# Keys and values of blocks 2 to 7 made transposed and turned back on TensorE, and fewer, moved looks at the weights

## The chip, the cores and the metric

The kernel runs on one core of one Trainium2 chip. The metric is the time of one execution on the device in microseconds (us). Three executions of the kernel before took 650.98, 651.08 and 651.11 us; the median is 651.08.

## The reference

One layer of attention without a softmax, and a feed-forward network with gates, each with a residual and a layer norm behind it, on 4096 tokens of width 256:

```
Q, K, V = x Wq^T, x Wk^T, x Wv^T              # width 64 each
energy  = K^T V                               # 64 x 64
out     = (Q energy) * sqrt(3/64) Wo^T
x       = layernorm(x + out)
h = silu(x W1^T * s1) * (x W2^T * s2)         # hidden width 1024
h = gelu(h H1^T * a1)
h = gelu(h H2^T * a2)
x = layernorm(x + (h W3^T) * s3)
```

The entries of W1, W2, H1, H2 and W3 are small whole numbers times a constant; all is float32.

## The kernel before

**Tiling.** The tokens are 8 blocks of 512, and two blocks make a pair. The two products with H1 and H2 are the bulk: each pair is multiplied by a Strassen-like scheme of 7 products per layer (`product`, L1338 in the profile), each 32 matmuls wide, whose left operands are sums of quarters of H (made once, from `unit` 0 to 7, by `combine` on GpSimd (POOL), stored to DRAM as `combos` and read back through three `ring` slots), and whose right operands are sums of quarters of the hidden values.

**Splitting.** A float32 operand goes to TensorE (PE) as two parts in a rounded type: the high part, rounded by ScalarE (ACT), and the low part, the rest, made by VectorE (DVE). So a value needs two matmuls against an exact weight. This holds only where a weight has no low bits; for that ACT looks at the low 16 bits of every weight (`bits`, which counts into `bits_done`), a small matmul sums what was found (`flag_sum`), DVE turns it into a flag (`flag_out`), and PE reads the flag and branches (`load_flag`) at seven points, the stages. `combine(i)` may overwrite unit i, so it waits for the look at it (`bits_of_whole(i)`); the sums are looked at too (`bits_of_sums(i)`).

**The front**, about the first 41 us: x^T arrives in 8 blocks `xT`. PE makes K and V of a block from x^T and `wkv` in plain float32 with the tokens as rows (`kv_products`, 8 instructions, L1181), DVE copies them out of PSUM (L1064), and PE adds K^T V into one bank (`energy`, L1189). Between them stand the products for Q with the split x (`q_pieces`, 4 matmuls of 512 columns for a block, L1164), whose high and low parts are made by ACT (`high_x`, L586) and DVE (`low_x`, L883). Then E Wo^T is formed (L1461) and split into T1s, block 0's attention is multiplied out (L1201), and its residual, statistics and norm go tile by tile over DVE, POOL (`inverse_deviation_tilewise`, L492 and L494), ACT (L637) or DVE (L1092), PE (L1213, a transpose) and again ACT and DVE (L631, L889: the split of x1T).

**First layer.** `l1(beta, ...)` makes 16 tiles of 4 matmuls (L1281) for a block; ACT applies silu to the even ones (L646), DVE multiplies with the odd ones (`gate`, L944). Behind tile 9 of block 0, PE transposes block 1, for which POOL's `inverse_deviation(0, 1)` (L463, L465) and DVE's `normalise` (L934) must be done.

**Order.** All order is written out by hand: each engine runs the list of its own block in program order, and the engines meet at semaphores. POOL's list is `combine(0)`, the tile-wise deviations, `combine(1)`, `inverse_deviation(0, 1)`, a wait for block 1's norm, `combine(2)` to `combine(4)`, then `differences(0, 0)` (L512, L522) and `further_differences` (L531, L534) of the hidden values. All loads are issued by SyncE's queue (SP) in one written order.

## Time and profile before

| | |
|---|---|
| median of 3 executions | 651.08 us |
| the profiled execution | 650.84 us, of which the span of the trace is 649.0 us |
| PE busy | 637.2 us (98%), clock granted 0.999 of full speed |
| DVE, ACT, POOL busy | 492.3, 408.6, 282.5 us |
| DMA | 103.91 MB moved; in the first four slices of 16 us 328, 397, 374 and 311 GB/s |

The spans of two views matter: the timeline (instructions in order of time, with the idle time of the engine ahead of each and what ended it) and the waits. PE runs almost without a pause after the first 43 us, so a microsecond that PE waits less in the front is worth a microsecond only if PE finds its operands that much earlier in all that follows.

### The profile page before, as it was taken

Reading aid. Unit: us, or ns where it says so; the run is one execution under the profiler, and the core shown is the slowest. Engines: PE = TensorE matmul, PEld = TensorE weight load, DVE = VectorE, ACT = ScalarE, POOL = GpSimd, SP = SyncE. Lnnn points to the kernel's source line nnn. Section 1 sums busy time; section 2 is a strip of 40 time slices with the busy share of each in tenths; the row PEclk is TensorE's granted clock in tenths of the full one; section 3 lists DMA queues with packets and bytes.
Section 4 is the critical chain, followed back from the end, with each engine's and each line's share of the span. In section 5 each row is a group of like instructions: output and inputs, shape, how many; then the busy total and the mean of one; then the engine's idle time right before and its main releaser. Section 6 shows DMA issues by size and latency. Waiting matters only on the chain.

```text
span 649.0 us, 9260 instructions
## 1 busy us (share of the span) xinstructions
PE 637.2 (98%) x3191; PEld 535.3 (82%) x3191; DVE 492.3 (76%) x721; ACT 408.6 (63%) x692; POOL 282.5 (44%) x226
## 2 busy tenths in 40 slices
PE   8989999999999999999999999999999999999995
PEld 6868788878879888888889888888879888888885
DVE  4677989989564997789655898698754899488476
ACT  5479689768671566558662657656763457566654
POOL 0367999493000762096000565078000367069025
PEclk9999999999999999999999999999999999999999
DMA  8998998973310046534330035634330015534201
GB/s 328 397 374 311 359 369 313 358 264 131 132 67 1 2 157 214 179 131 138 130 123 1 0 98 181 256 123 154 131 130 1 1 25 186 179 130 156 105 1 68
DMA packets 24371, 103.91 MB, mean 160 GB/s; under 512 B 2224, under 2 KB 3312, under 8 KB 16496
## 3 DMA queue, kind: packets, MB, share of 16 engines
q1 hardware_dynamic: 24032, 102.98, 44.7%
q8 instruction: 30, 0.49, 0.3%
q10 hardware_dynamic: 288, 0.26, 0.1%
q14 instruction: 21, 0.17, 0.1%
HBM read 87.51 MB, written 23.07 MB: 170 GB/s over the span
## 4 chain that ended last, share of the span: by engine, by line
PE 88%; DVE 5%; issue 2%; ACT 2%; DMA 1%; POOL 1%; SPq 0%; POOLq 0%; ACTq 0%; DVEq 0%
PE ps L1338 56%; PE ps L1281 17%; PE ps L1407 8%; DVE R L950 3%; PE ps L1181 2%; PE ps L1213 1%; PE ps L1164 1%; DMA xT<-in_xT 1%; PE ps L1430 1%; PE ps L1201 1%; ACT R L682 1%; PE ps L1189 1%; ACT junk L575 1%; POOL rstd L494 0%; DVE st L921 0%
## 5 line engine op out<-in xcount | busy, mean ns | idle before, releaser
L1338 PE MATMUL ps<-R,ring 128*128 128x512 f32 x1792 | 410.2, 390 | 0.2 <-DVE fsum L870 0.2
L1338 PEld LDWEIGHTS ps<-R,ring 128*128 128x128 f32 x1792 | 335.2, 188 | 69.9 <-DVE fsum L870 0.6
L950 DVE TENSOR_TENSOR R<-quarter,R 128x512 fp32r<-128x512 f32 x284 | 262.7, 948 | 57.3 <-ACT R L682 56.9
L682 ACT CAST R<-quarter 128x512 fp32r<-128x512 f32 x284 | 173.2, 617 | 30.3 <-POOL quarter L522 12.3
L1281 PE MATMUL ps<-x1T,w 128*128 128x512 f32 x512 | 119.1, 391 | 1.1 <-issue 0.4
L728 ACT ACTIVATE quarter<-U,sc 128x512 f32<-128x512 f32 x96 | 69.5, 724 | 73.0 <-DVE U L977 28.6
L1281 PEld LDWEIGHTS ps<-x1T,w 128*128 128x128 f32 x512 | 95.4, 188 | 22.6 <-ACT sg L646 1.2
L512 POOL TENSOR_TENSOR quarter<-quarter,quarter 128x512 f32<-128x512 f32 x32 | 50.5, 1578 | 94.8 <-ACT quarter L728 88.1
L463 POOL TENSOR_TENSOR ve<-mv,eps 128x4 f32<-128x4 f32 x14 | 5.6, 402 | 182.4 <-DVE mv L927 182.4
L646 ACT ACTIVATE sg<-ps,sc 128x512 f32<-128x512 f32 x64 | 44.2, 690 | 63.4 <-PE ps L1281 63.2
L698 ACT COPY U<-ps 128x512 f32<-128x512 f32 x96 | 56.3, 586 | 29.4 <-PE ps L1338 29.3
L944 DVE SCALAR_TENSOR_TENSOR quarter<-ps,sc,sg 128x512 f32<-128x512 f32 x64 | 47.6, 746 | 22.2 <-PE ps L1281 12.2
L522 POOL TENSOR_TENSOR quarter<-quarter,quarter 128x512 f32<-128x512 f32 x32 | 49.5, 1548 | 16.7 <-DVE quarter L944 12.8
L1407 PEld LDWEIGHTS ps<-w,R 128*128 128x128 f32 x448 | 54.7, 192 | 0.7 <-DVE R L950 0.2
L1407 PE MATMUL ps<-w,R 128*128 128x256 f32 x448 | 55.1, 283 | 0.0
L534 POOL TENSOR_TENSOR quarter<-quarter,quarter 128x512 f32<-128x512 f32 x32 | 50.0, 1590 | 0.0
L531 POOL TENSOR_TENSOR quarter<-quarter,quarter 128x512 f32<-128x512 f32 x32 | 48.8, 1555 | 0.0
L934 DVE TENSOR_SCALAR xr<-xr,mv,rstd 128x256 f32<-128x256 f32 x52 | 35.5, 742 | 4.2 <-POOL rstd L465 4.2
L971 DVE TENSOR_TENSOR U<-ps,U 128x512 f32<-128x512 f32 x32 | 22.0, 691 | 14.5 <-PE ps L1338 14.5
L728 ACT ACTIVATE quarter<-ps,sc 128x512 f32<-128x512 f32 x32 | 22.3, 696 | 12.4 <-PE ps L1338 12.4
L977 DVE TENSOR_TENSOR U<-ps,U 128x512 f32<-128x512 f32 x32 | 21.8, 684 | 8.6 <-PE ps L1338 8.5
L905 DVE TENSOR_TENSOR U<-ps,s3b 128x1024 f32<-128x1024 f32 x7 | 8.5, 1219 | 21.6 <-PE ps L1407 21.6
(85 smaller groups left out, 392.8 us busy)
## 6 DMA issues: line engine op xcount, KB each, us to landing
ring<-combos SPq DMA_DIRECT2D x56, 1024.0 KB, 5.0
combos<-unit SPq DMA_DIRECT2D x8, 1024.0 KB, 7.3
unit<-in_h1T SPq DMA_DIRECT2D x4, 1024.0 KB, 14.1
xr<-in_x_rows SPq DMA_DIRECT2D x8, 512.0 KB, 5.8
unit<-in_h2T SPq DMA_DIRECT2D x4, 1024.0 KB, 9.5
xT<-in_xT SPq DMA_DIRECT2D x7, 512.0 KB, 8.7
out<-xr SPq DMA_DIRECT2D x7, 512.0 KB, 3.3
w<-w_dram SPq DMA_DIRECT2D x3, 1024.0 KB, 7.8
```

The lines of the kernel that those rows point to most:

```text
L512: nc.gpsimd.tensor_tensor(x12[:, c, :], x12[:, c, :], x11[:, c, :], ALU.subtract).then_inc(t_done, 1)
L522: nc.gpsimd.tensor_tensor(t2[:, c, :], x22[:, c, :], x12[:, c, :], ALU.subtract).then_inc(t_done, 1)
L531: nc.gpsimd.tensor_tensor(x11[:, c, :], t2[:, c, :], x11[:, c, :], ALU.subtract).then_inc(t_done, 1)
L534: nc.gpsimd.tensor_tensor(x21[:, c, :], x21[:, c, :], t2[:, c, :], ALU.subtract).then_inc(t_done, 1)
L682: nc.scalar.copy(R[slot_of(p, u)][:, 0, c, :], quarter[operand_home(p, u)][:, c, :]).then_inc(hi_done, 1)
L698: nc.scalar.copy(U[:, 1 if i == 2 else 0, j, :], ps[:, B + j, :]).then_inc(cp_done, 1)
L728: nc.scalar.activation(quarter[dst][:, j, :], src, ACT.Gelu, scale=sc[:, 2 + l, chunk:chunk + 1]).then_inc(gelu_done, 1)
L944: nc.vector.scalar_tensor_tensor(quarter[dst][:, j % KH, :], ps[:, base + (2 * j + 1) % 4, :], sc[:, 1, j:j + 1], sg[:, j % 2, :], ALU.mul ...
L950: nc.vector.tensor_tensor(r[:, 1, c, :], quarter[operand_home(p, u)][:, c, :], r[:, 0, c, :].bitcast(f32), ALU.subtract).then_inc(lo_done, 1)
L1281: last = nc.tensor.matmul(ps[:, base + t % 4, :], w, view(x1T[beta % 2][:, part, c, :]), start=n == 0, stop=n == 2 * EC - 1)
L1338: last = nc.tensor.matmul(ps[:, bank + j, :], w, view(R[slot_of(p, u)][:, part, k, :]), start=n in (0, 1, 5) and k == 0 and part == 0, sto ...
L1407: last = nc.tensor.matmul(rows_of(b)[:, q, :], view(slot[:, part, k, q * P:(q + 1) * P]), w, start=first and k == 0 and part == 0 and q % ...
```

## The change

1. K and V of blocks 2 to 7 are made transposed: 4 matmuls of 512 columns against the split x (`kv_transposed`, in three PSUM banks by `KV_BANK`), copied to SBUF by ACT (`copy_kvt`), turned by 4 transposes on PE (`kv_turned`), copied out by DVE as before. A rounded copy `wkvr` of the weights is made, and ACT also looks at the low bits of `wkv`.
2. w1 and w2 are looked at in two instructions of 2048 elements instead of four of 1024.
3. One tile of block 0 is normalised by ACT instead of two; the flag of stage 1 is taken behind DVE's norms; PE does the four transposes of block 0 in one piece, runs 5 matmuls on zeros ahead of them, and both halves of block 1's attention come behind the branch.
4. The looks at units 1, 2 and 3 and the sums move in ACT's list. The rows of block 0 are loaded ahead of w1 and w2.

```diff
-BIT_ORDER = [("wq", 0), ("whole", 0), *[("w12", i) for i in range(4)], ("whole", 1), ...
+BIT_ORDER = [("wkv", 0), ("wq", 0), ("whole", 0), ("w12", 0), ("w12", 1), ("whole", 1), ...
-ACT_TILES = (2, 3)
+ACT_TILES = (1, 3)
+KV_BANK = (0, 1, 3, 0, 1, 3, 0, 1)
+WARM_MIDDLE = 5
@@ SP
             load_unit(0)
+            load_rows(0)
             load_w12(0)
             load_w12(1)
-            load_rows(0)
             load_unit(1)
@@ ACT
+            def copy_kvt(f):
+                act.wait_ge(kvt_ready, f - 1)
+                nc.scalar.copy(kvT[f % 2][:, :], ps[:, KV_BANK[f], :]).then_inc(kvt_out, 1)
...
+            act.wait_ge(wkv_in, 16)
+            bits_of_wkv()
+            nc.scalar.copy(wkvr[:, :, :], wkv[:, :, :]).then_inc(wkv_rounded, 1)
...
-            for f in range(4):
+            for f in range(5):
                 high_x(f)
+            copy_kvt(2)
             hi_of_q(0)
-            high_x(4)
+            high_x(5)
+            copy_kvt(3)
             hi_of_q(1)
-            high_x(5)
+            high_x(6)
+            copy_kvt(4)
             raw_q(2)
-            high_x(6)
+            high_x(7)
             raw_q(3)
-            high_x(7)
+            for f in range(5, NB):
+                copy_kvt(f)
             bits_of_whole(0)
-            bits_of_w12(0)
-            bits_of_w12(1)
+            raw_q(4)
             act.wait_ge(t1_ready, 1)
             nc.scalar.activation(T1s[:, 0, :], ps[:, 3, 0:E], ACT.Copy, scale=CTX_SCALE).then_inc(t1_hi, 1)
-            raw_q(4)
-            bits_of_w12(2)
-            bits_of_w12(3)
-            raw_q(5)
+            for i in range(2):
+                bits_of_w12(i)
             for q in range(ACT_TILES[0]):
                 normalise_tile(0, 0, q, q + 1, tile_norm[0])
-            bits_of_whole(1)
+            raw_q(5)
             raw_q(6)
             hi_of_transposed(0, 6)
             raw_q(7)
@@ ACT, silu(0, j) and silu(1, j)
-                if j == 0:
-                    bits_of_whole(2)
-                if 2 <= j <= 3:
-                    bits_of_sums(0, range(j - 2, j - 1))
+                if j <= 1:
+                    bits_of_whole(j + 1)
+                if j == 3:
+                    bits_of_sums(0, range(1))
...
                 if j == 5:
-                    bits_of_whole(3)
+                    bits_of_sums(0, range(1, 2))
             for j in range(HC):
                 silu(1, j, A)
-                if j <= 1:
-                    bits_of_sums(1, range(j, j + 1))
-                if j == 2:
+                if j == 0:
+                    bits_of_whole(3)
+                if 1 <= j <= 2:
+                    bits_of_sums(1, range(j - 1, j))
+                if j == 3:
                     bits_of_whole(4)
-                if 3 <= j <= 4:
-                    bits_of_sums(2, range(j - 3, j - 2))
+                if 5 <= j <= 6:
+                    bits_of_sums(2, range(j - 5, j - 4))
@@ DVE
-                nc.vector.tensor_copy(kv[f % 2][:, :], ps[:, f % 2, :]).then_inc(kv_out, 1)
-                if f < NB - 1:
-                    low_x(f)
+                nc.vector.tensor_copy(kv[f % 2][:, :], ps[:, KV_BANK[f], :]).then_inc(kv_out, 1)
                 if f == 0:
+                    low_x(0)
                     flag_out(0)
-                if 1 <= f <= 2:
-                    lo_of_q(f - 1)
+                elif f == 1:
+                    low_x(2)
+                    low_x(1)
+                    low_x(3)
+                    low_x(4)
+                    lo_of_q(0)
+                elif f <= 4:
+                    if f == 4:
+                        lo_of_q(1)
+                    low_x(f + 3)
...
-            normalised_tilewise(0, 0, attention_residual, lambda: flag_out(1))
+            normalised_tilewise(0, 0, attention_residual)
+            flag_out(1)
@@ PE
+            def kv_transposed(f, view):
+                if f > 2:
+                    pe.wait_ge(kv_out, f - 2)
+                for part in range(2):
+                    pe.wait_ge(*((xhi_done, f + 1) if part == 0 else (xlo_done, n_xlo(f))))
+                    for c in range(EC):
+                        x = xhi[f % 4][:, c, :] if part == 0 else tiles_of(xlo[f])[:, c, :, :]
+                        last = nc.tensor.matmul(ps[:, KV_BANK[f], :], wkvr[:, c, :] if view is exact else wkv[:, c, :], view(x),
+                                                start=part == 0 and c == 0, stop=part == 1 and c == 1)
+                last.then_inc(kvt_ready, 1)
+
+            def kv_turned(f):
+                pe.wait_ge(kvt_out, f - 1)
+                for q in range(TPB):
+                    last = nc.tensor.transpose(ps[:, KV_BANK[f], q * P:(q + 1) * P], kvT[f % 2][:, q * P:(q + 1) * P], ident[:, :])
+                last.then_inc(kv_ready, 1)
...
                 for f in range(2, NB):
-                    kv_products(f)
-                    energy(f - 1)
+                    kv_transposed(f, view)
                     if f <= Q_BETWEEN:
                         q_pieces(range(4 * (f - 1), 4 * f), view)
+                    if f == 2:
+                        energy(1)
+                    else:
+                        kv_turned(f - 1)
+                    if f >= 4:
+                        energy(f - 2)
...
-                q_pieces(range(23, 28), view)
+                q_pieces(range(24, 28), view)
+                pe.wait_ge(q_raw, 2)
+                keep_clock(WARM_MIDDLE, 7)
+                q_pieces(range(28, 32), view)
+                for q in range(TPB - 1):
+                    transposed_first(q)
                 pe.wait_ge(tile_sum[0], 1)
                 flag_sum(1)
-                pe.wait_ge(q_raw, 2)
-                transposed_first(0)
-                q_pieces(range(28, 30), view)
-                transposed_first(1)
-                q_pieces(range(30, 32), view)
+                transposed_first(TPB - 1).then_inc(tr_ready, 1)
@@ first_l1
-                transposed_first(2)
                 attention_half(0)
-                transposed_first(3).then_inc(tr_ready, 1)
                 attention_half(1).then_inc(op_ready, 1)
```

How the instructions stand. On PE, in the middle of the front, before (xT_106 is block 4, kv_90 and kv_91 the two copies of keys and values in turn):

```order
L1181 MATMUL ps<-wkv,xT_106 128x128 x8
L1189 MATMUL ps<-kv_91 64x64 x4
L1164 MATMUL ps<-xhi_113,wqr 128x512 x2
L1164 MATMUL ps<-xlo_117,wqr 128x512 x2
L1181 MATMUL ps<-wkv,xT_107 128x128 x8
L1189 MATMUL ps<-kv_90 64x64 x4
```

and in the changed kernel (L1223 the transposed keys and values, xhi_113 with xlo_121 block 4 and xhi_116 with xlo_120 block 3; L1230 turns them, L1237 is the energy):

```order
L1223 MATMUL ps<-xhi_113,wkvr 128x512 x2
L1223 MATMUL ps<-xlo_121,wkvr 128x512 x2
L1195 MATMUL ps<-xhi_116,wqr 128x512 x2
L1195 MATMUL ps<-xlo_120,wqr 128x512 x2
L1230 MATMUL ps<-ident,kvT_104 128x128 x4
L1237 MATMUL ps<-kv_90 64x64 x4
L1223 MATMUL ps<-xhi_114,wkvr 128x512 x2
```

Eight float32 instructions of 128 columns became four of 512 and four transposes, and a block's energy is one step further behind its product.

On ACT, around the first silu, before (unit_123 is unit 1, unit_124 unit 2; w_49 is w1 and w2; x1T_63 the split of block 0, sg the silu):

```order
L575 ACTIVATE junk,lowf<-w_49 128x1024 x2
L611 COPY q_stage_97<-ps 128x512
L637 ACTIVATE xr<-xr,shift,rstd_85 128x256 x2
L575 ACTIVATE junk,lowf<-unit_123 128x1024
L611 COPY q_stage_98<-ps 128x512
L631 CAST x1T_63<-ps 128x512 x2
L611 COPY q_stage_99<-ps 128x512
L646 ACTIVATE sg<-ps,sc 128x512
L575 ACTIVATE junk,lowf<-unit_124 128x1024
```

and in the changed kernel (unit_126 is unit 1, unit_127 unit 2):

```order
L586 ACTIVATE junk,lowf<-w_49 128x2048 x2
L656 ACTIVATE xr<-xr,shift,rstd_85 128x256
L630 COPY q_stage_97<-ps 128x512
L630 COPY q_stage_98<-ps 128x512
L650 CAST x1T_63<-ps 128x512 x2
L630 COPY q_stage_99<-ps 128x512
L665 ACTIVATE sg<-ps,sc 128x512
L586 ACTIVATE junk,lowf<-unit_126 128x1024
L665 ACTIVATE sg<-ps,sc 128x512
L586 ACTIVATE junk,lowf<-unit_127 128x1024
```

The look at unit 1 has moved from ahead of the split of block 0 to behind the first silu.

On ACT, in the later silus of block 0 and the first of block 1, before (unit_125 is unit 3, R_59 a high part of the hidden values):

```order
L646 ACTIVATE sg<-ps,sc 128x512
L682 CAST R_59<-quarter_52 128x512
L575 ACTIVATE junk,lowf<-unit_125 128x1024
L646 ACTIVATE sg<-ps,sc 128x512
L682 CAST R_59<-quarter_52 128x512
L646 ACTIVATE sg<-ps,sc 128x512
L682 CAST R_59<-quarter_52 128x512
L646 ACTIVATE sg<-ps,sc 128x512
```

and in the changed kernel (beside_133 belongs to unit 0, unit_128 is unit 3, unit_126 unit 1):

```order
L665 ACTIVATE sg<-ps,sc 128x512
L701 CAST R_59<-quarter_52 128x512
L586 ACTIVATE junk,lowf<-beside_133 128x512
L665 ACTIVATE sg<-ps,sc 128x512
L701 CAST R_59<-quarter_52 128x512
L665 ACTIVATE sg<-ps,sc 128x512
L701 CAST R_59<-quarter_52 128x512
L665 ACTIVATE sg<-ps,sc 128x512
L586 ACTIVATE junk,lowf<-unit_128 128x1024
L665 ACTIVATE sg<-ps,sc 128x512
```

The look at unit 3 has moved from behind silu 5 of block 0 to behind silu 0 of block 1.

## Rows read from the trace of the kernel before

**Rows 1.** Waits of PE, the longest in the front: engine, line, releaser; us in total, times, longest.

```profile
PE ps L1213 <- ACT xr L637: 1.1, 1, 1.1
```

**Rows 2.** Timeline of PE's loads in the front: start us, duration, engine, line.

```profile
24.66 1.86 PEld L1181 LDWEIGHTS ps<-wkv,xT 128*128 128x128 f32 x16
...
26.64 0.54 PEld L1189 LDWEIGHTS ps<-kv 128*64 128x64 f32 x8
...
27.25 1.86 PEld L1181 LDWEIGHTS ps<-wkv,xT 128*128 128x128 f32 x16
```

**Rows 3.** Timeline, PE's transposes of block 1.

```profile
50.76 1.02 PEld L1213 LDWEIGHTS ps<-ident,xr 128*128 128x128 f32 x8
...
51.75 4.40 PEld L1281 LDWEIGHTS ps<-x1T,w 128*128 128x128 f32 x20
```

**Rows 4.** Timeline, end of the front, ACT, POOL, DVE and PE.

```profile
18.86 0.59 ACT L611 COPY xr<-ps 128x512 f32<-128x512 f32 x1 [1.99 <-PE ps L1164]
...
24.22 1.06 ACT L575 ACTIVATE junk<-unit 128x1024 uint8<-128x1024 uint16 x1 [0.31 <-DMA unit<-in_h1T]
25.55 1.56 POOL L452 TENSOR_TENSOR beside<-unit 128x512 f32<-128x512 f32 x1 [23.87 <-ACT junk L575]
...
33.98 0.42 DVE L1097 TENSOR_TENSOR xr<-ps,xr 128x256 f32<-128x256 f32 x1 [0.55 <-PE ps L1201]
...
35.16 0.19 POOL L492 TENSOR_TENSOR ve<-mv,eps 128x1 f32<-128x1 f32 x1 [3.15 <-DVE mv L1087]
...
38.51 0.62 POOL L494 TENSOR_TENSOR rstd<-ve,nhalf 128x1 f32<-128x1 f32 x1
...
39.31 1.41 POOL L452 TENSOR_TENSOR beside<-unit 128x512 f32<-128x512 f32 x1 [0.19 <-ACT junk L575]
```

**Rows 5.** Timeline, first layer of block 0.

```profile
42.46 1.68 PEld L1281 LDWEIGHTS ps<-x1T,w 128*128 128x128 f32 x8 [0.41 <-DVE x1T L889]
43.06 0.69 ACT L646 ACTIVATE sg<-ps,sc 128x512 f32<-128x512 f32 x1 [0.99 <-PE ps L1281]
43.52 1.30 POOL L458 TENSOR_TENSOR unit<-unit 128x512 f32<-128x512 f32 x1
...
46.60 0.20 POOL L463 TENSOR_TENSOR ve<-mv,eps 128x4 f32<-128x4 f32 x1 [1.78 <-DVE mv L927]
...
46.88 1.02 POOL L465 TENSOR_TENSOR rstd<-ve,nhalf 128x4 f32<-128x4 f32 x1
...
48.29 1.37 DVE L934 TENSOR_SCALAR xr<-xr,mv,rstd 128x256 f32<-128x256 f32 x4
```

**Rows 6.** Timeline, ACT and POOL around units 3 and 4, and PE's and ACT's wait on POOL.

```profile
55.94 1.29 POOL L452 TENSOR_TENSOR beside<-unit 128x512 f32<-128x512 f32 x1 [0.80 <-ACT junk L575]
...
59.01 1.90 ACT L575 ACTIVATE junk<-unit 128x2048 uint8<-128x2048 uint16 x1
...
60.71 1.63 POOL L458 TENSOR_TENSOR unit<-unit 128x512 f32<-128x512 f32 x1
...
63.95 1.30 POOL L452 TENSOR_TENSOR beside<-unit 128x512 f32<-128x512 f32 x1 [1.60 <-ACT junk L575]
...
69.71 1.28 POOL L512 TENSOR_TENSOR quarter<-quarter,quarter 128x512 f32<-128x512 f32 x1
...
82.61 0.62 ACT L682 CAST R<-quarter 128x512 fp32r<-128x512 f32 x1 [2.04 <-POOL quarter L522]
```

**Rows 7.** Timeline of PE and DVE in the first hidden layer.

```profile
77.84 34.75 PE L1338 MATMUL ps<-R,ring 128*128 128x512 f32 x152
...
93.11 8.32 DVE L950 TENSOR_TENSOR R<-quarter,R 128x512 fp32r<-128x512 f32 x5 [0.20 <-ACT R L682]
```

**Rows 8.** SP's issue of the ring load at 99.71, with its time to landing.

```profile
L336 SPq DMA_DIRECT2D ring<-combos x1: 1187/1187/1187, 99.7 to 99.7; - x1
...
DMA to landing us min/median/max: 8.7/8.7/8.7
```

**Rows 9.** Timeline, PE's first matmuls, on zeros.

```profile
1.17 3.17 PE L1195 MATMUL ps<-zeros 128*128 128x512 bf16 x7 [1.17 <-DVE zeros L1059]
```

More of the change, by code:

```diff
@@ L33 @@
 BITS = 3 * KH
-BIT_ORDER = [("wq", 0), ("whole", 0), *[("w12", i) for i in range(4)], ("whole", 1), ("whole", 2), ("sums", 0), ("whole", 3),
+BIT_ORDER = [("wkv", 0), ("wq", 0), ("whole", 0), ("w12", 0), ("w12", 1), ("whole", 1), ("whole", 2), ("sums", 0), ("whole", 3),
              ("sums", 1), ("whole", 4), ("sums", 2), ("sums", 3), ("whole", 5), ("sums", 4),
@@ L149, in build @@
         wqr = over("wqr", q_at + 2 * 8192 + 1024, [P, EC, 2 * D], f32r)
+        wkvr = over("wkvr", q_at + 2 * 8192 + 2048, [P, EC, 2 * D], f32r)
+        kvT = [over(f"kvT{i}", q_at + 8192 + 1024 + 2048 * i, [P, BLK]) for i in range(2)]
         xT = [over(f"xT{f}", r_at + 4096 * f, [P, TPB * E]) for f in range(NB)]
@@ L575, in bits, with bits_of_wkv @@
                 nc.scalar.activation(dst, src, ACT.Copy, accum_out=lowf[:, s, col:col + 1]).then_inc(bits_done, 1)
+            def bits_of_wkv():
+                bits(low_halves(wkv[:, :, :].rearrange("p c n -> p (c n)")), 0, BITS - 2)
+            def copy_kvt(f):
+                act.wait_ge(kvt_ready, f - 1)
+                nc.scalar.copy(kvT[f % 2][:, :], ps[:, KV_BANK[f], :]).then_inc(kvt_out, 1)
             def bits_of_wq():
@@ L1077, in _, with normalised_tilewise @@
                                            ALU.mult, ALU.subtract).then_inc(t1_lo, 1)
-            def normalised_tilewise(ln, b, add, between=None):
+            def normalised_tilewise(ln, b, add):
                 y = xr[:, b % 4, :].rearrange("p (t e) -> p t e", e=E)
@@ L1087, in normalised_tilewise @@
                     nc.vector.bn_aggr(mv[ln][:, ln, q, :], st[ln][:, ln, q, :]).then_inc(tile_aggr[ln], 1)
-                if between is not None:
-                    between()
                 for q in range(ACT_TILES[ln], TPB):
@@ L1222, in flag_sum @@
             def flag_sum(s):
-                pe.wait_ge(bits_done, n_bits(*(("wq", 0), ("w12", 3), ("whole", KH - 1), ("sums", KH - 1), ("whole", NU - 1),
+                pe.wait_ge(bits_done, n_bits(*(("wq", 0), ("w12", 1), ("whole", KH - 1), ("sums", KH - 1), ("whole", NU - 1),
                                                ("sums", NU - 1), ("w3", 1))[s]))
                 if s < FLAGS - 1:
-                    row, col, n = ((0, BITS - 1, 1), (0, 0, 4), (1, 0, KH), (1, KH, 2 * KH), (2, 0, KH), (2, KH, 2 * KH))[s]
+                    row, col, n = ((0, BITS - 2, 2), (0, 0, 2), (1, 0, KH), (1, KH, 2 * KH), (2, 0, KH), (2, KH, 2 * KH))[s]
                     at = lowf[:, row, col:col + n]
@@ L1449, in front @@
                 pe.wait_ge(wq_rounded, 1)
+                pe.wait_ge(wkv_rounded, 1)
                 q_pieces(range(4), view)
                 for f in range(2, NB):
-                    kv_products(f)
-                    energy(f - 1)
+                    kv_transposed(f, view)
                     if f <= Q_BETWEEN:
                         q_pieces(range(4 * (f - 1), 4 * f), view)
+                    if f == 2:
[4 more added lines that the diff above has]
+                        energy(f - 2)
+                kv_turned(NB - 1)
+                energy(NB - 2)
+                q_pieces(range(16, 18), view)
                 energy(NB - 1)
                 pe.wait_ge(cst_in, 16 * NCST)
-                q_pieces(range(16, 18), view)
+                q_pieces(range(18, 20), view)
                 pe.wait_ge(et_out, 1)
@@ L1462, in front @@
                                  start=True, stop=True).then_inc(t1_ready, 1)
-                q_pieces(range(18, 23), view)
+                q_pieces(range(20, 24), view)
                 pe.wait_ge(qlo_done, 1)
```

17 lines of the change are left out of this document (9 added, 8 removed).

## The prediction

> **What bounds the kernel now.** I read the waits of PE first. After its first few microseconds PE hardly waits: the longest of its waits is 1.1 us, in the front, for a normalised tile [rows 1]. PE is busy for 98% of the span, so the kernel is a row of PE's instructions with a short front ahead of it, and a change of the front is worth what is left of it where PE next finds its operands late. I then read the timeline of the front by engine, and from there followed POOL, the engine with the fewest busy microseconds, through the first hidden layer, since two others wait for it in this trace: ACT waits 2.04 us for a difference made by POOL at 82.61 [rows 6], and POOL waits for looks by ACT at 55.94 and 63.95 [rows 6]. The reader is to see that POOL's list stands close behind ACT's looks and close ahead of ACT's roundings. The profiled execution took 650.84 us (span 649.0), 0.24 below the median of 651.08. I sum against 650.84 and add 0.24 at the end. About 1.3 us (0.2%) is what can be told from no change.
>
> **Front: PE's own work.** Two passes over K and V of a block are 2.59 us apart without Q between them, 1.98 us of it keys and values (24.66 to 26.64) and 0.61 the energy [rows 2]. Now a block takes 4 matmuls of 512 columns; 152 of them take 34.75 us, 0.229 us each [rows 7], so 0.91 us, and 4 transposes. Eight transposes stand 0.99 us ahead of the next load [rows 3], 0.124 each, so 0.50 us. Per block 1.98 - 0.91 - 0.50 = 0.57 us, over 6 blocks 3.4 us. The added steps are on ACT 6 copies of 0.59 us [rows 4] and the look and rounding of `wkv`, which fall into time when ACT waited for x^T or for PE; the new order lets the energy of a block run one block later, which hides the two copies of each block behind the next block's product. I take these at nothing; were one copy of each block exposed, 6 x 0.59 = 3.5 us would take all back.
>
> The transposes rest on [rows 3]. The Trainium skill, "TensorE: Matmul & The Clock Gate", on the PE-mode transpose, gives about 275 ns for one in a kernel. If that were the step from one to the next, the 24 would take 6.6 us instead of 3.0 and the 3.4 us would be gone; in this trace the step is 0.124 us, and I go by it.
>
> **Front: what is late next.** The sum of block 0's first tile starts at 33.98 and its deviation at 35.16, where POOL had been waiting 3.15 us [rows 4]. With the front 3.4 us shorter the statistics would be there at 31.7. But `combine(0)` now begins later: it waits for ACT's look at unit 0, at 24.22 before, and POOL starts 1.33 us behind a look's start [rows 4]. Now the last three copies of keys and values stand ahead of it (the last, by the order, not before PE has made block 7, at about 24.8), so the look begins about 25.4 and POOL at 26.7. `combine(0)` ended 3.15 us ahead of 35.16, at 32.0, so it took 6.46; `combine(1)` took 44.82 - 39.31 = 5.51 [rows 4, 5]. I take 5.9: POOL is free at 32.6, and POOL, not PE, is what is late. From the first deviation to the end of the last were 39.13 - 35.16 = 3.97 us [rows 4]; one tile less goes to ACT, so POOL makes one shift less, of about 0.35 us. Last deviation at 32.6 + 3.6 = 36.2, 2.9 us earlier than 39.13. From there to the fourth load of the first layer were 42.46 - 39.13 = 3.33 us [rows 4, 5]. Now the flag comes behind DVE's norms and all eight attention matmuls of block 1 behind the branch: between 2.9 (the branch is free) and 4.1 us; I take 3.75. The fourth load then stands at 40.0, 2.5 us earlier than 42.46. The five matmuls on zeros (1.1 us) lie in the wait for POOL, the shorter looks at w1 and w2 (two of 1.90 for four of 1.06 [rows 4, 6]) end ahead of the first shift, and loading block 0's rows first makes w1 and w2 later by 0.5 MB at 374 GB/s, 1.4 us, which no one waits for. Bounds of this gain: 3.5 if POOL is as fast as in `combine(1)` and the branch free, 1.4 if neither.
>
> **Block 1's norm takes it back.** The look at unit 1 stood ahead of the first layer; POOL began `combine(1)` at 39.31 [rows 4]. Now it stands behind silu 0 of block 0, which waits for the first tile. Silu 0 goes to 43.06 - 2.5 = 40.6, the look starts 0.6 behind, 41.2, POOL 1.33 later, 42.5, and `combine(1)` ends 5.51 later, at 48.0. Only then, by POOL's order, comes block 1's deviation: 46.60 to 47.90 is 1.30 us [rows 5], so 49.4, and DVE's norm takes 1.37 [rows 5]: 50.8. Before, PE's transposes of block 1 started at 50.76 [rows 3] and no wait ended there. Now PE comes to them at 50.76 - 2.5 = 48.3 and waits 2.5 us. Queued behind the transposes on PE is all of the first layer; behind the norm on DVE are the gates from 3 on, which PE needs only from two tiles after the transposes on. So at 51 us nothing is left of the front: 0.0, bounds -1.1 to +0.8, which are those of the front since the distance from silu 0 to the norm is fixed at 10.2 us.
>
> **The look at unit 3 costs more.** It stood behind silu 5 of block 0, and POOL started unit 3 at 55.94; now it takes the place behind silu 0 of block 1, where the row at 59.01 stands [rows 6]. POOL starts unit 3 at 59.01 + 1.33 = 60.34, 4.4 us later. Unit 3 took 62.34 - 55.94 = 6.40 us and unit 4 took 69.71 - 63.95 = 5.76 [rows 6]; 1.60 us of idle time between them goes. The differences of the hidden values start at 72.55 instead of 69.71, 2.84 us late. Their four pairs ran from 69.71 to 82.57, the first of them ahead of DVE's low parts; shifted into these they may take 0.7 more. I take 3.2, bounds 1.6 (both units at 5.51) and 4.8. ACT waited for the last of them at 82.61, so ACT is late by the same 3.2, and behind it on ACT stand the raw q of two blocks, a look, the table load and the gelus with the roundings for product 3; DVE's low parts follow these. They are not hidden: the first of the five low parts at 93.11 (8.32/5 = 1.66 us, so ready at 94.77) is the last operand of product 3's first tile; PE needs it at matmul 78 counted from 77.84, 77.84 + 78 x 0.229 = 95.67 [rows 7]. Slack 0.90 us, so PE waits 2.3 us. Next, SP issues the ring load at 99.71 behind a wait for ACT's look at the sums of unit 4, which is late by 3.2 as well; it landed 8.7 us later, at 108.41 [rows 8], and PE needs it at matmul 136, at 108.93. Slack 0.52, so the total wait grows to 3.2 - 0.52 = 2.7 us. From 118 on POOL's row shows idle time again, and PE's pace carries the rest unchanged.
>
> DVE and POOL slow each other: POOL's step takes 1.29 us alone and 1.63 at 60.71, beside DVE's low parts [rows 6]. The Trainium skill, "SBUF — State Buffer", on who interferes with whom, says a DVE instruction with two SBUF inputs and a GpSimd instruction that reads SBUF exclude each other for a whole instruction. By that, with all eight steps of units 3 and 4 blocked for a low part of about 0.7 us, the differences would be 1.65 + 5.6 = 7.2 us late and the kernel near 657.8; by the row a step loses 0.34, and I go by the row.
>
> **Sum.** 650.84 + 0.0 + 2.7 = 653.5; with the 0.24, 653.8 us.
>
> **Rivals.** *The front gain is kept.* One place decides: block 1's transposes. If POOL starts unit 1 before about 40.1 (the look being counted earlier than I read, or the norm not behind it), PE doesn't wait there, and if POOL also catches up before product 3, the 2.5 us stay: 650.84 - 2.5 + 0.24 = 648.6; with a part of the later wait up to 649.9. For it: POOL had 1.78 us idle before 46.60. Against: the order of the rows on ACT, in which unit 1 stands behind silu 0. 17%.
> *POOL is fast.* With fewer DVE instructions beside it, all its steps take 1.3 us: `combine(0)` is over early, the front gains 3.2 and block 1's wait leaves 0.7 of it; the differences are 1.6 late, less 0.5 is 1.1. 650.84 - 0.7 + 1.1 + 0.24 = 651.5, no change. For it the 1.29 us steps from 49.75 on; against it the 1.63 ones beside low parts, which stand there too. 23%.
> *My forecast*, 651.9 to 655.3 as its own range: 53%.
> *The clock falls.* The granted clock was 0.999 with no wait over 1.2 us in the front; now there are two of 2.3 to 2.5. At the lower level a matmul of 512 columns took 3.17/7 = 0.45 us [rows 9] instead of 0.229, so each 3 us at that level cost 1.5 more. Two such stretches: 653.8 + 3.0 = 656.8. 7%.
>
> **The numbers.** Range 649.6 to 656.0. Faster by over 0.2%: the first rival and a little of the second, 0.19. Within: most of the second and the low edge of the forecast, 0.22. Slower: 0.59.
>
> **What would show it.** Right: energy of block 7 near 27 instead of 30.20; unit 0 on POOL from about 26.7; the fourth load of the first layer near 40.0; a wait of PE of about 2.5 us for DVE's norm ahead of block 1's transposes, near 48 to 51; unit 3 on POOL from about 60.3; a wait of PE for a low part near 95 and for the ring near 111. Wrong: PE runs through 50 us without a wait, or POOL starts the differences before 71; then the time is below 651. A front longer than before (energy of block 7 after 29) would mean that copies by ACT are exposed.

## The result and the profile after

The changed kernel takes 653.46 us, median of 7 executions (652.67 to 655.78), against 651.08 before (650.98 to 651.24, 7 executions): ratio 1.0041, 95% interval 1.0031 to 1.005. It is 2.4 us slower. The forecast was 653.8 in a range of 649.6 to 656.0.

The profiled execution took 653.81 us, its span is 652.0 and its mean clock 0.994; the one before had 650.84, 649.0 and 0.999. So the two traces are 3.0 us apart, a little more than the medians.

The longest waits of PE after the change (engine, line, releaser; us in total, times, longest). L1261 are the transposes, L1386 the products, L1249 the attention:

```profile
PE ps L1261 <- DVE xr L960: 2.1, 1, 2.1
PE ps L1386 <- ACT U L717: 1.8, 1, 1.8
PE ps L1249 <- issue: 1.3, 1, 1.3
```

In [rows 1] the longest was 1.1. Two new waits of about 2 us stand in the places that the prediction named, and a third of 1.3 behind the branch. The timeline of the front and of the first layer, where the rows answer to [rows 2 to 5]:

```profile
26.00 1.06 ACT L586 ACTIVATE junk<-unit 128x1024 uint8<-128x1024 uint16 x1
27.33 1.28 POOL L463 TENSOR_TENSOR beside<-unit 128x512 f32<-128x512 f32 x1 [25.66 <-ACT junk L586]
28.32 0.68 PE L1237 MATMUL ps<-kv 128*64 128x64 f32 x8
32.97 0.19 POOL L503 TENSOR_TENSOR ve<-mv,eps 128x1 f32<-128x1 f32 x1 [0.26 <-DVE mv L1119]
36.27 0.61 POOL L505 TENSOR_TENSOR rstd<-ve,nhalf 128x1 f32<-128x1 f32 x1
37.47 0.14 DVE L897 TENSOR_SCALAR flag<-fsum 1x1 int32<-1x1 f32 x1
39.15 1.19 PE L1249 MATMUL ps<-T1s,qs 128*128 128x256 f32 x8 [1.33 <-issue]
40.06 8.95 PEld L1329 LDWEIGHTS ps<-x1T,w 128*128 128x128 f32 x40
41.37 0.69 ACT L665 ACTIVATE sg<-ps,sc 128x512 f32<-128x512 f32 x1 [1.94 <-PE ps L1329]
41.95 1.05 ACT L586 ACTIVATE junk<-unit 128x1024 uint8<-128x1024 uint16 x1
43.23 1.31 POOL L463 TENSOR_TENSOR beside<-unit 128x512 f32<-128x512 f32 x1 [6.36 <-ACT junk L586]
48.89 1.02 POOL L476 TENSOR_TENSOR rstd<-ve,nhalf 128x4 f32<-128x4 f32 x1
49.95 1.38 DVE L960 TENSOR_SCALAR xr<-xr,mv,rstd 128x256 f32<-128x256 f32 x4 [3.29 <-POOL rstd L476]
51.48 1.06 PE L1261 MATMUL ps<-ident,xr 128*128 128x128 f32 x8 [2.05 <-DVE xr L960]
```

Read it in two halves. Down to 40.06 everything is earlier than before: the energy of block 7 at 28.32 instead of 30.20, the first deviation at 32.97 instead of 35.16 [rows 4], the first layer, whose loads begin at 40.06 and go on every 0.23 us, so that the fourth stands at about 40.76, 1.7 us ahead of 42.46 [rows 5]. Then POOL stands idle for 6.36 us until silu 0 and the look behind it are over, and from there the chain look, unit 1, deviation, norm, transposes runs without a gap. The loads of block 1's transposes were followed by the first layer's next load at 51.75 [rows 3]; that load now stands at 52.27, so PE is 0.5 us late where it had been 1.7 early.

The second half of the story, in the same view:

```profile
60.83 1.61 POOL L463 TENSOR_TENSOR beside<-unit 128x512 f32<-128x512 f32 x1 [3.52 <-ACT junk L586]
67.02 1.47 POOL L463 TENSOR_TENSOR beside<-unit 128x512 f32<-128x512 f32 x1
72.97 1.75 POOL L523 TENSOR_TENSOR quarter<-quarter,quarter 128x512 f32<-128x512 f32 x1
85.78 0.62 ACT L701 CAST R<-quarter 128x512 fp32r<-128x512 f32 x1 [1.85 <-POOL quarter L533]
96.14 0.58 ACT L717 COPY U<-ps 128x512 f32<-128x512 f32 x1
96.27 3.17 DVE L976 TENSOR_TENSOR R<-quarter,R 128x512 fp32r<-128x512 f32 x2 [0.21 <-ACT R L701]
96.77 20.02 PE L1386 MATMUL ps<-R,ring 128*128 128x512 f32 x80 [1.78 <-ACT U L717]
```

Against [rows 6]: unit 3 at 60.83 instead of 55.94, the differences at 72.97 instead of 69.71, 3.26 us late; ACT's rounding behind the last difference at 85.78 instead of 82.61, 3.17 late; product 3, whose first matmul is the 73rd counted from 77.84 [rows 7], at 96.77 instead of 94.30, 2.47 late. What the last row also shows is that 80 matmuls took 20.02 us, 0.250 each, where [rows 7] has 0.229. Windows of the same trace say why (stretch and its length, busy us of each engine with its instructions, then the granted clock, DMA share and GB/s):

```profile
96.00:98.00 2.00, 1.23 (x5) 1.06 (x6) 1.79 (x3) 2.00 (x5) 2.00 (x2) 0.95 1.01 394
98.00:100.00 2.00, 2.00 (x7) 1.51 (x6) 2.00 (x2) 2.00 (x3) 2.00 (x2) 0.50 0.27 107
100.00:102.00 2.00, 2.00 (x8) 1.60 (x7) 1.96 (x2) 2.00 (x7) 1.92 (x2) 0.70 0.01 4
102.00:104.00 2.00, 2.00 (x11) 1.65 (x10) 2.00 (x2) 2.00 (x5) 1.90 (x2) 1.00 0.54 119
```

Behind the wait PE ran from 98 to 100 at 0.50 of full speed, the lower of its two levels, 1.2 GHz instead of 2.4, and came back during the next two microseconds. By these rows that is 2 x 0.50 + 2 x 0.30 + 2 x 0.05 = 1.7 us of PE's work. PE is then 4.2 us behind (its small matmul for the next flag is at 116.71, before at 112.52). Small stalls that the kernel before had vanish under this delay: at 180 us PE is 3.35 us behind, at its last product 2.95 (637.58 against 634.63). So 1.2 us come back, which leaves the 3.0 of the spans.

### The profile page after: what moved, and what is told of

It reads as the page before. It is cut to its first block, busy times and chain, and to the rows that moved or that the text cites. A ratio compares the mean times of both kernels' runs of the same rounds, so it can differ in the third digit from the quotient of the medians.

```text
span 652.0 us, 9170 instructions
## 1 busy us (share of the span) xinstructions
PE 636.4 (98%) x3148; PEld 532.6 (82%) x3148; DVE 490.4 (75%) x722; ACT 411.3 (63%) x696; POOL 280.9 (43%) x225
## 4 chain that ended last, share of the span: by engine, by line
PE 84%; POOL 1%; issue 1%; DVE 1%; ACT 0%; POOLq 0%; ACTq 0%; DVEq 0%
PE ps L1386 59%; PE ps L1329 13%; PE ps L1455 8%; PE ps L1249 1%; PE ps L1261 1%; PE ps L1478 1%; POOL quarter L542 1%; POOL rstd L505 0%; DVE U L991 0%; DVE R L976 0%; POOL shift L497 0%; POOL ve L503 0%; ACT R L701 0%; POOLq L91 0%; ACT U L717 0%
## 5 line engine op out<-in xcount | busy, mean ns | idle before, releaser
L1386 PE MATMUL ps<-R,ring 128*128 128x512 f32 x1792 | 411.7, 391 | 1.8 <-ACT U L717 1.8
L1386 PEld LDWEIGHTS ps<-R,ring 128*128 128x128 f32 x1792 | 336.4, 188 | 71.8 <-ACT U L717 2.2
L970 DVE SCALAR_TENSOR_TENSOR quarter<-ps,sc,sg 128x512 f32<-128x512 f32 x64 | 47.5, 746 | 20.9 <-PE ps L1329 11.8
L463 POOL TENSOR_TENSOR beside<-unit 128x512 f32<-128x512 f32 x8 | 12.2, 1520 | 37.0 <-ACT junk L586 35.5
```

Of the source, the lines that this page charges most:

```text
L970: nc.vector.scalar_tensor_tensor(quarter[dst][:, j % KH, :], ps[:, base + (2 * j + 1) % 4, :], sc[:, 1, j:j + 1], sg[:, j % 2, :], ALU.mul ...
L1386: last = nc.tensor.matmul(ps[:, bank + j, :], w, view(R[slot_of(p, u)][:, part, k, :]), start=n in (0, 1, 5) and k == 0 and part == 0, sto ...
```

## The experiments

Each kernel was executed 5 to 12 times beside the kernel before, which took 651.17, 651.09 and 651.20 us in the three sets (the first four kernels below, the next four, the last three). "Ratio" is to it, with the 95% interval. All kernels but the fourth start from the changed one.

**The moved looks put back.** In the first the look at unit 1 goes back ahead of the first layer; in the second those from unit 3 on go back to where they stood; in the third both.

```diff
+            bits_of_whole(1)                     # first and third
             hi_of_transposed(0, 6)
...
-                if j <= 1:
-                    bits_of_whole(j + 1)
+                if j == 0:
+                    bits_of_whole(2)
@@ silu(0, 5), silu(1, j)                        # second and third
+                    bits_of_whole(3)
             for j in range(HC):
                 silu(1, j, A)
-                if j == 0:
-                    bits_of_whole(3)
...
```

> The changed kernel with the look at unit 1 put back ahead of the split of block 0. Theory (the look behind silu 0 holds POOL's unit 1, and with it block 1's norm): POOL starts unit 1 near 37.5 instead of 43.23, PE's wait of 2.1 us ahead of block 1's transposes goes, the wait of 1.8 us at product 3 stays, and the time is 2.1 us less: about 651.3. Rival (the transposes wait because DVE's statistics or the attention behind the branch come late): the wait stays above 1 us and the time falls by less than 1 us.

Measured: 650.87 us (650.12 to 652.01, 11 executions), ratio 0.9998, 0.9989 to 1.0007.

> The changed kernel with the looks from unit 3 on back in their places of before (unit 3 behind silu 5 of block 0, unit 4 behind silu 2 of block 1). Theory: POOL starts the differences near 70.5 instead of 72.97, PE doesn't wait at product 3, the granted clock stays at 1.00 from 97 to 103 us, and the wait (1.9), the clock (1.7 in the profiled run) go: about 650.8, and the spread between executions shrinks. Rival (product 3 waits because all of ACT's list is later by its added work): the wait shrinks by less than half; above 652.

Measured: 650.74 us (650.29 to 652.64, 11), ratio 0.9998, 0.9989 to 1.0007.

> Both edits together: what is left of the change is the transposed keys and values, the two looks at w1 and w2, the tile of block 0 and the order around the branch. Theory (the two waits are separate costs that add up): no wait of PE at either place, the front's gain of 1.7 us at the fourth load of the first layer arrives at the end: about 649.2, under the kernel before. Rival (a later place takes the gain, such as the ring load or the gates): 650.5 to 651.5.

Measured: 649.13 us (648.30 to 651.65, 11), ratio 0.9977, 0.9966 to 0.9988.

All three came within 0.5 us of what was expected. So each set of moved looks costs: from 649.13 the time goes to 650.74 with unit 1's late (1.6 us), to 650.87 with the later ones late (1.7), and to 653.46 with both (4.3). The timeline of the first of the three, POOL and PE:

```profile
36.91 1.26 POOL L463 TENSOR_TENSOR beside<-unit 128x512 f32<-128x512 f32 x1 [0.44 <-ACT junk L586]
48.85 1.03 PE L1262 MATMUL ps<-ident,xr 128*128 128x128 f32 x8
94.12 20.04 PE L1387 MATMUL ps<-R,ring 128*128 128x512 f32 x80 [1.80 <-ACT U L717]
```

and of the second:

```profile
50.73 1.06 PE L1260 MATMUL ps<-ident,xr 128*128 128x128 f32 x8 [2.04 <-DVE xr L959]
77.64 31.23 PE L1385 MATMUL ps<-R,ring 128*128 128x512 f32 x136
109.14 3.88 PE L1385 MATMUL ps<-R,ring 128*128 128x512 f32 x16 [0.26 <-issue]
```

With unit 1 started at 36.91, PE comes to block 1's transposes at 48.85 without a wait, and keeps its wait of 1.80 at product 3. With the later looks back it is the other way round: the wait of 2.04 at the transposes stays, and PE runs through product 3. Each wait belongs to one set of looks and comes without the other. The costs do not simply add up: together they are 1.0 us more than the sum of the two alone. A part of this shows in the traces: with looks back PE is early enough to meet another wait, at 109.28 (0.58, below) with both back and at 109.14 (0.26) with the later ones back, and it meets none there in the changed kernel.

**Before, with the look at unit 3 late.** That one look alone, in the kernel before.

```diff
-                if j == 5:
-                    bits_of_whole(3)
             for j in range(HC):
                 silu(1, j, A)
+                if j == 0:
+                    bits_of_whole(3)
```

> The kernel before with one edit: the look at unit 3 moved from behind silu 5 of block 0 to behind silu 0 of block 1. Theory: POOL starts unit 3 near 60.3, the differences near 72.5, PE waits about 2 us at product 3, and the clock may fall behind it: 652.5 to 655. Rival (the look is harmless without the new front): within 0.5 us of the kernel before.

Measured: 653.53 us (653.05 to 654.05, 5), ratio 1.0039, 1.0026 to 1.0052. The size was as expected, the place was not:

```profile
60.32 1.91 ACT L575 ACTIVATE junk<-unit 128x2048 uint8<-128x2048 uint16 x1
60.37 1.61 POOL L452 TENSOR_TENSOR beside<-unit 128x512 f32<-128x512 f32 x1 [5.15 <-ACT junk L575]
62.23 0.67 ACT L646 ACTIVATE sg<-ps,sc 128x512 f32<-128x512 f32 x1
62.94 0.75 DVE L944 SCALAR_TENSOR_TENSOR quarter<-ps,sc,sg 128x512 f32<-128x512 f32 x1 [2.11 <-ACT sg L646]
67.41 2.79 PE L1281 MATMUL ps<-x1T,w 128*128 128x512 f32 x11 [1.32 <-DVE quarter L944]
72.55 1.47 POOL L512 TENSOR_TENSOR quarter<-quarter,quarter 128x512 f32<-128x512 f32 x1
```

POOL's rows came as expected (60.37, 72.55), but here ACT had two looks in a row behind silu 0 (59.09 and 60.32), silu 1 began only at 62.23, the gates on DVE were late and PE waited 1.32 us for one at 67.41. PE started its row of 152 matmuls 1.7 us late (79.55 instead of 77.84) and lost 0.8 more in it, where its loads wait 1.1 us in all for ACT's copies of the banks of product 3. One look moved behind three silus costs 2.4 us in this kernel. In the changed one the set that has this look costs 1.7 us alone and 2.7 beside the late unit 1; which wait shows it depends on what else stands on ACT.

**The wait filled.** Eight matmuls whose result is overwritten run where PE waits for product 3's bank.

```diff
+                    if L == 0 and n == 3 and j == 0:
+                        ...                       # waits for its operands only
+                        for _ in range(8):
+                            nc.tensor.matmul(ps[:, A, :], ..., start=True, stop=True)
                     bank_free(p, l, n, j)
```

> The changed kernel with eight more matmuls of 512 columns (1.83 us at full clock, results unused, in a free bank) just ahead of product 3, where PE waits 1.8 us for ACT's copy and where the granted clock fell to 0.63 and 0.80 behind the wait. Theory (the clock falls because of the idle time, and costs up to 1.7 us on top of the wait): product 3 starts when it did (near 96.8), PEclk stays 1.00 behind it, the time falls by 0.5 to 1.7 us (median of executions with and without a fall) and the spread between executions, 652.7 to 655.8, shrinks to under 1 us. Rival (the fall has nothing to do with the wait): the time stays at 653.5 with the same spread, or rises.

Measured: 654.23 us (652.78 to 654.99, 6), ratio 1.0048, 1.0036 to 1.006. The expectation of a gain failed. In the profiled execution the fill did what it should there:

```profile
90.00:97.00 7.00, 7.00 (x31) 5.52 (x30) 6.69 (x7) 5.41 (x10) 7.00 (x5) 1.00 1.04 413
97.00:103.00 6.00, 6.00 (x26) 4.62 (x25) 6.00 (x5) 6.00 (x11) 5.84 (x4) 1.00 0.31 98
```

The clock stayed at 1.00 behind product 3, and that execution took 653.39. Yet the six executions had mean clocks of 0.994 to 0.997, and none reached the 0.998 and 0.999 that two of the unfilled kernel's seven have. The two traces say where the gain went:

```profile
114.91 0.19 PE L1278 MATMUL ps<-lowf,ones 128*1 128x4 f32 x2
141.66 16.63 PE L1393 MATMUL ps<-R,ring 128*128 128x512 f32 x72 [0.29 <-DVE fsum L895]
183.19 14.75 PE L1329 MATMUL ps<-x1T,w 128*128 128x512 f32 x64 [0.59 <-issue]
```

and, without the fill,

```profile
116.71 0.19 PE L1278 MATMUL ps<-lowf,ones 128*1 128x4 f32 x2
183.71 14.76 PE L1329 MATMUL ps<-x1T,w 128*128 128x512 f32 x64 [0.43 <-issue]
```

With the fill PE was 1.80 us ahead at its next flag, but only 0.52 at 183 us, since small waits stood in between that the late PE of the changed kernel doesn't meet. By these two traces the fall behind product 3 costs about 0.5 us of time and not 1.7, less than the executions spread. Why the median with the fill isn't lower even by that stays open: no other execution's clock was seen in time, and the two ratios, 1.0048 and 1.0041, can't be told apart.

**Two places that the traces pointed to.** In the version with all looks back, PE still waits 1.35 us behind the branch and 0.58 ahead of product 5 (the row at 109.28 below). The first of these kernels puts both halves of block 1's attention ahead of the branch; the second issues the sixth ring load ahead of block 2's rows and of one copy from DRAM to DRAM (`relay_hidden`).

```diff
                 transposed_first(TPB - 1).then_inc(tr_ready, 1)
+                attention_half(0)
+                attention_half(1).then_inc(op_ready, 1)
@@ SP, the second kernel
             load_rows_late(3)
+            load_ring(5)
             load_rows_late(2)
             relay_hidden(1, 1)
-            load_ring(5)
```

> The kernel with both looks back, and both halves of block 1's attention ahead of the branch of stage 1 instead of behind it. Theory (from the flag to the next matmul PE stands 1.3 to 1.4 us, which those 8 matmuls can fill): the first matmul of the first layer comes 0.7 to 1.0 us earlier, then DVE's low part of block 0 ends the wait; the time falls by 0.7: about 648.4. Rival (PE's sequencer can't run ahead, the branch takes its 1.5 us from the last matmul on): no gain, 649.1.

Measured: 647.84 us (647.43 to 648.27, 5), ratio 0.9951, 0.9938 to 0.9964.

> The kernel with both looks back, and SP issues the sixth ring load ahead of block 2's rows instead of behind them, so that it no longer waits for ACT's look at the sums of unit 4. Theory (PE's wait of 0.6 us at 109.3, ahead of product 5, which the profile puts down to issue, is for this load): the wait goes and the time falls by 0.5: about 648.6. Rival (the wait has another cause, such as the bank): it stays, 649.1.

Measured: 648.69 us (648.30 to 649.63, 5), ratio 0.9964, 0.9951 to 0.9977. The timeline of the version with the looks back:

```profile
38.79 1.39 PE L1249 MATMUL ps<-T1s,qs 128*128 128x256 f32 x8 [1.35 <-issue]
39.98 10.70 PE L1329 MATMUL ps<-x1T,w 128*128 128x512 f32 x40
109.28 3.91 PE L1386 MATMUL ps<-R,ring 128*128 128x512 f32 x16 [0.58 <-issue]
```

and with the halves ahead of the branch:

```profile
37.18 1.20 PE L1249 MATMUL ps<-T1s,qs 128*128 128x256 f32 x8
38.86 9.37 PE L1329 MATMUL ps<-x1T,w 128*128 128x512 f32 x40 [0.48 <-ACT x1T L650]
```

The attention fills the time in which PE waited behind the branch, and the first layer starts 1.1 us earlier. The idle time at 109.28 has no releaser in the row, but it is the ring's: the load was issued at 99.7 and landed 9.5 us later, at 109.2, and with the load issued at 93.22 the idle time is gone. This is the wait that the prediction's [rows 8] stood for. Alone, the earlier load is worth nothing that can be told from no change: its five executions (648.30 to 649.63) lie where the faster six of the eleven of the version beside it do (648.30 to 649.13, median 648.6). Against those six the halves ahead of the branch are worth 0.8 us, not 1.3; the rest of the 1.3 is that none of its five was a slower one.

**Without the five matmuls on zeros,** in the version with the looks back (`WARM_MIDDLE = 0`).

> The kernel with both looks back, without the five matmuls on zeros. Theory (they lie in a wait for a tile's sum and only keep PE busy): the first layer starts at the same time, PE waits 1.1 us more near 34; if they keep the clock up, the granted clock falls in more executions between 36 and 46 us and the median rises by 0.3 to 1 us. Rival (they do nothing): 649.1 and the same spread.

Measured: 649.07 us (648.13 to 650.47, 11), ratio 0.9972, 0.9963 to 0.998, against 649.13 with them. PE waits 2.00 us instead of 0.90 ahead of the last Q products and starts the first layer as before. They do nothing that can be measured.

**Keys and values as before,** in the version with the looks back: `kv_products(f)` and `energy(f - 1)` for every block, no `copy_kvt`, DVE's old order of `low_x`.

```diff
-                    kv_transposed(f, view)
+                    kv_products(f)
+                    energy(f - 1)
                     if f <= Q_BETWEEN:
                         q_pieces(range(4 * (f - 1), 4 * f), view)
-                    ...                           # kv_turned, energy(f - 2)
```

> The version with both groups of looks put back, but keys and values of blocks 2 to 7 made as before (rows of tokens, plain float32, no copies by ACT, no transposes; the low parts in DVE's order of before). Theory: the transposed keys and values carry the whole gain of the front; PE reaches block 0's attention some 2 us later, the first deviation, at 32.58 in the version with the looks back, waits for its tile again and comes near 34.7, and the time goes from 649.13 to about 651.2. Rival: POOL's combination of unit 0, which ended at 32.3 there, bounds the front however fast PE is, and without the ACT copies the look at unit 0 is earlier; then the time stays within 0.6 of 649.1.

Measured: 651.09 us (650.10 to 653.01, 12), ratio 0.9999, 0.999 to 1.0008. POOL in this kernel:

```profile
25.80 1.27 POOL L463 TENSOR_TENSOR beside<-unit 128x512 f32<-128x512 f32 x1 [24.12 <-ACT junk L586]
27.15 2.31 POOL L465 TENSOR_TENSOR unit<-unit 128x512 f32<-128x512 f32 x1
35.32 0.19 POOL L503 TENSOR_TENSOR ve<-mv,eps 128x1 f32<-128x1 f32 x1 [3.14 <-DVE mv L1107]
```

The deviation is late again, at 35.32, and POOL waits 3.14 us for it as in [rows 4]. The time is that of the kernel before: the transposed keys and values (with the order of DVE's `low_x` that goes with them) are worth 1.96 us, the whole gain of the version with the looks back, and without them the rest of the change is worth nothing that can be measured. This closes the sum: 2.0 us gained by them, 4.3 lost by the moved looks, which leaves the 2.3 to 2.4 us of the change.

**All together.** First both later corrections, then the same with w1 and w2 looked at in four instructions again.

```diff
-            for i in range(2):
+            for i in range(4):
                 bits_of_w12(i)                    # and 1024 elements each
```

> The version with both groups of looks put back (649.13 us), with both of the later corrections at once: the halves of block 1's attention ahead of the branch (alone 1.29 us faster) and the sixth ring load issued earlier (alone 0.44). Theory: the two act at different places and add up, 649.13 - 1.29 - 0.44 = 647.4, with no idle time of PE ahead of product 5. Rival: with PE 1.3 us earlier the ring load, whose own time is bound to its issue and not to PE, is late even from the earlier place; then 647.8, with some idle time near 106.

Measured: 647.35 us (647.00 to 648.73, 5), ratio 0.9944, 0.9931 to 0.9957: 3.8 us faster than before and 6.1 faster than the change as it was made. PE has no idle time ahead of product 5 any more, and the earlier load has brought 0.5 us more than the halves alone.

> The version with both later corrections, with w1 and w2 looked at in four instructions of 1024 elements instead of two of 2048. Theory: four of 1.06 us for two of 1.90 are 0.44 us more of ACT ahead of the one tile that ACT normalises; that tile's copy stood at once behind the looks, so up to 0.4 us of it shows, 647.4 to 647.9. Rival: ACT has room there, nothing changes (within 0.2 of the version beside it).

Measured: 647.49 us (646.95 to 647.68, 5), ratio 0.994, 0.9927 to 0.9953. Two looks or four make no difference that can be measured; ACT had the room.

## Why the prediction was right

The result lies 0.3 us from the forecast, and the mechanism was the one forecast, each half confirmed by undoing it. The terms were less exact than the sum, and one wait had another releaser than was said.

- *PE's own work in the front, 3.4 us.* Between the first product of block 1 and the energy of block 7 lie 20.12 us with the looks back and 22.99 with keys and values as before, 2.87 less. A block without Q between takes 2.16 us (22.13 to 24.29 in the changed kernel) where it took 2.59, so 0.43 less instead of 0.57: its four matmuls took 1.02 us and not 0.91, the four transposes 0.53 and not 0.50. The ACT copies are hidden, as taken. The forecast that the energy of block 7 would be near 27 had this term too large, and left out that two more Q matmuls now stand ahead of it; it was 28.32.
- *POOL is late next.* The first deviation was forecast at 32.6 and stood at 32.97, where POOL had been free 0.26 us; `combine(0)` took 5.4 us, not 5.9, but its look began at 26.00 instead of 25.4. PE and POOL come to this point together. The last deviation was over at 36.88 (forecast 36.2).
- *The first layer 2.5 us earlier.* It was 1.7. Of the 0.76 that lack, 0.68 are the last deviation, over at 36.88; the way from there to the fourth load took 3.88 us against the 3.75 taken. The branch is in that way: the flag was finished at 37.61, PE's work ahead of the branch ended at 37.82, and the first matmul behind it came at 39.15, after 1.33 us of idle time.
- *Block 1's norm takes it back.* Right in place, order and size: a wait of 2.05 (forecast 2.5), for DVE's norm. From silu 0 to the end of the norm were 9.96 us, forecast 10.2 and fixed. The net at 51 us was +0.5 instead of 0.0, since the front was 0.8 later than forecast and this distance 0.24 shorter. The first kernel settles it: only the look at unit 1 was put back, and only this wait went.
- *The look at unit 3.* Unit 3 at 60.83 (60.34), the differences 3.26 us late and ACT's last rounding 3.17 (3.2 for both). Right. The prediction weighed two ways in which DVE and POOL slow each other, and went by 0.34 us for a step of POOL. The size held; the rows show the mechanism more exactly (in the last section).
- *Product 3 waits 2.3 us for a low part.* PE was 2.47 us late there, of which 1.78 a new wait; the size holds, the releaser was wrong. PE waited for ACT's copy of the bank, 96.14 to 96.72. The row for it before:

```profile
92.98 0.58 ACT L698 COPY U<-ps 128x512 f32<-128x512 f32 x1
```

  There it ended 0.74 us ahead of product 3, closer than the 0.90 that I gave the low part. The low part that I had named is the first of the row at 96.27. It was ready at about 97.8 and is needed at the seventh matmul, 98.14, so it was late by nearly as much: without the bank's wait PE would have reached it at about 96.4 and waited 1.4 us (an estimate from these rows). The two limits stand 0.4 us apart. I had looked only for the operands of the first tile, not for the bank that it writes. Both hang on ACT's 3.2 us, so the sum didn't suffer; that they stand so close is luck.
- *The ring, 0.4 us.* Absent here: the load was issued 3.2 us late, at 102.86, and landed 9.2 us later, at 112.06, but PE itself was 4 us late by then. The limit is real, and shows as soon as PE is early (0.26 and 0.58 us of idle time at 109, 0.42 at 106.66 with the halves ahead of the branch), but a delay of PE and a delay of the load don't add up.
- *The clock, a rival with 7%.* It came beside the forecast, not in its place. The profiled execution lost 1.7 us of PE's work behind product 3, about 0.5 of it in the end. The changed kernel's two executions with a mean clock of 0.998 and 0.999 took 652.96 and 652.67, those with 0.996 and 0.997 653.46 and 653.31, the one with 0.991 654.93, and the two with 0.994 655.78 and 653.81. So the kernel with little lost clock stands at about 652.8 (an estimate from two executions), 1.0 below the forecast: no ring wait (0.4 to 0.5), and a part of PE's delay given back by the stalls of before. The median is 0.7 above that; the clock may be the reason, but where the other executions lost it was not seen. The two errors cancel in part, and that the result lies within 0.3 us of the forecast is luck. The rival's price came from [rows 9], where a matmul took 0.45 us; the granted clock recorded over that row is 1.00, so only its pace says that it is the lower level.
- *The rivals.* That the gain is kept would have needed unit 1 before 40.1; it started at 43.23. That POOL is fast came true for units 0 and 1 (5.4 us each), but didn't matter for block 1, whose chain starts with silu 0.

## What to carry to other kernels

A front made shorter is worth nothing until the next engine that the work passes through is shorter too; find the chain that starts latest (here a look by ACT, then POOL, then a norm) and see where the same change has put its first link. A check or any other side work on an engine in order is not free where it stands if a third engine waits for it: moving looks by a few instructions cost 1.6 to 2.7 us each time. A stall or a lower clock on the busiest engine costs less than its length where small waits stand behind it: 1.8 us won at one place were 0.5 at the end. And when a wait is forecast, list everything that the first instruction behind it needs, the place it writes to as well as its operands.

## What the runs showed of the hardware

- Time follows the mean granted clock in some kernels and hardly in others. With the looks back, the six executions at 0.997 to 0.999 lie between 648.30 and 649.13, and the five at 0.994 to 0.996 between 650.03 and 651.65. With only unit 1's look back, the four at 0.994 took 650.87 to 651.68 and the four at 0.998 and 0.999 650.12 to 650.91. One reason is that the mean takes in the end of the span, where PE has nothing left to do: with the later looks back every stretch of 10 us up to 640 stood at 1.00, PE ended at 642.07, and the clock was 0.50 from 644 to 648, enough for a mean of 0.996.
- A wait of about 2 us doesn't always bring the clock down. Behind 2.05 us at the transposes of the changed kernel it stayed at 1.00; behind 1.78 at product 3 it fell to 0.50, and behind the 1.80 of the first experiment it fell too (0.83 from 90 to 100). In the version with the looks back it fell between 36 and 46 us, behind waits of 0.90 and then 1.35, which the version with only unit 1's look back has too (0.89 and 1.32) at 1.00:

```profile
36.00:46.00 10.00, 8.52 (x40) 6.81 (x39) 5.70 (x17) 4.77 (x9) 5.59 (x5) 0.83 1.05 354
```

  With the halves ahead of the branch it was 1.00 there, and all 15 executions of the three kernels that have them so had 0.996 or more. That they avoid the fall is likely, not shown: the kernel with only the ring load moved had 0.996 or more in all five as well.
- From a finished flag to PE's first matmul behind the branch that reads it passed 1.5 to 1.6 us in the changed kernel (37.61 to 39.15), in the three with looks put back, with the fill and without the zeros. With keys and values as before it was 0.94 (40.94 to 41.88), and in the kernel before 1.08. What makes the difference is not shown.
- A step of POOL on 512 columns took 1.28 us alone. One that starts inside a DVE subtraction with both inputs in SBUF ended 1.1 to 1.2 us behind the end of that, and such a subtraction of 512 columns that starts inside a step of POOL ended about 0.55 us behind the end of the step. Rows after the change:

```profile
62.52 1.47 POOL L465 TENSOR_TENSOR unit<-unit 128x512 f32<-128x512 f32 x1
62.87 1.67 DVE L976 TENSOR_TENSOR R<-quarter,R 128x512 fp32r<-128x512 f32 x1
64.07 1.63 POOL L467 TENSOR_TENSOR unit<-unit 128x512 f32<-128x512 f32 x1
```

  The step ends at 63.99 and the subtraction at 64.54; the next step ends at 65.70, 1.16 behind it. So the two exclude each other for a whole instruction, and what a step loses is the rest of the one that it runs into: 0.3 to 0.5 us beside low parts of 512 columns, 1.0 beside one of 1024 (2.31 us, from 27.15, beside DVE's 27.12 to 28.34, with keys and values as before). The 5.6 us that the prediction weighed had each of eight steps lose a whole low part. DVE's multiplications that read PSUM (L970) cost POOL nothing: the step at 51.41 took 1.28 beside two of them.
- 24 transposes of 128 columns in the front have a mean record of 0.274 us, yet four of them in a row take 0.60 to 0.66 us from the first start to the last end, since each starts before the one ahead of it has ended.
